# Sending tokens to per-expert regions during the gates instead of gathering them in the routed stage of a one-core ViT tower with a mixture of experts

## The chip, the cores and the metric

One core of one Trainium2 chip runs the whole program in one launch. The metric is the device time of that core in microseconds (us); lower is better. PE is the matrix engine, ACT the activation engine, DVE the vector engine, POOL the GpSimd engine, SP the engine that only issues DMAs here.

## The reference, cut to what matters

64 images give 64 x 49 = 3136 tokens of width 128. After a patch embedding, a layer norm and an S4 convolution comes the part that the change touches, a feed-forward layer with 2 shared and 8 routed experts (hidden width 512). Each token goes to its two best experts.

```python
hs = gelu(einsum('td,nfd->ntf', t, sw1) + sb1)            # 2 shared experts, all tokens
shared = einsum('ntf,ndf->td', hs, sw2) + sb2.sum(0)
logits = t @ gate_w.T + gate_b
probs = softmax(logits); top_v, top_i = top_k(probs, 2)
cw = zeros_like(probs).at[arange(T)[:, None], top_i].add(top_v)
hr = gelu(einsum('td,efd->etf', t, rw1) + rb1)            # 8 routed experts
oe = einsum('etf,edf->etd', hr, rw2) + rb2
out = h + shared + einsum('etd,te->td', oe, cw)
```

## The kernel before, in words

Tokens are held 98 to a group (two images, `PAIR`), 32 groups (`NPAIR`); four groups make a chunk of 392 tokens (`GT`), and there are 8 chunks (`NG`). All engines have a program of their own, written out by hand, and meet through semaphores alone; each engine runs its own in order.

The feed-forward layer is a list of 48 units in a fixed order (`ORDER`, lines 77 to 83). 16 are shared units (one chunk by one shared expert), 32 are routed units, called blocks here: 256 slots that belong to one expert (`NB` = 32, `BLK` = 256). The first 12 units are shared; then come the blocks, with one more shared unit behind every sixth block.

PE works one unit ahead (L1523 to L1550): in step q it does the up-projection of unit q+1 (`up`, L1443), transposes the gathered tokens of the block after that (`transpose_in`, L1508), and then does the down-projection of unit q (`down_shared` L1462, `down_routed` L1473). ACT does the gelu between them (L765). DVE copies the transposed tokens out (`keep_x`, L1145) and adds the bias to a block's result (`rows_out`, L1151, tile `og`). A down-projection of block i waits for `og` of block i-1.

The tokens' way before the change: the normalised tokens `ym` of each chunk are stored to a DRAM table `yd` by SP (`store_y`, L469). In the steps up to q = 3, PE multiplies each chunk with the gate weights (`gate`, L1430). When all eight chunks are done, DVE computes softmax, picks the two best experts and gives each (token, expert) pair a slot (`gate_logits`, `gate_probs`, `gate_second`, `sort_places`, L1033 to L1115), with one pair of matmuls in between (`count_places`, L1493). Slots are then turned into index lists by one-hot matmuls (`one_hots` L1117, `invert` L1500, `slot_tokens` L1128): `take` says which token a slot takes, `give` to which row of the DRAM table `rd` its result goes. POOL then gathers 128 tokens per indirect DMA, two per block, up to four blocks ahead (`gather`, L605), and scatters the results, again two per block (`scatter`, L613). POOL's order is: gathers of blocks 0 to 3, then for each i the gathers of block i+4 and the scatters of block i (L620 to L628). A gather waits until its buffer's earlier tokens have been transposed, a scatter for `og`.

SP loads each block's expert weights from a copy in SBUF, `wba` (up, 258 KB) and `wbb` (down, 320 KB), three blocks ahead (`load_weights`, L474). Before `wbb` of block i+3 it waits for `og` of block i. At the end SP loads the routed rows back (`load_routed`), ACT and DVE weigh and add them (`scale_routed`, `combine`), and SP stores the output.

Before its first up-projection, DVE waits for constants that POOL makes (`sort_constants`, L578).

## Time and profile before

| what | us |
|---|---|
| median of three runs | 507.42 (505.32 to 509.38) |
| the profiled execution, own time | 508.58 |
| its span, first to last instruction | 506.8 |
| PE busy | 386.9 (76%) |
| ACT busy | 208.2 (41%) |
| POOL busy | 193.4 (38%) |
| DVE busy | 183.7 (36%) |

The span is what the rows below divide; the own time lies 1.8 us above it. The shares are averages over stages with different limits: patch embedding and convolution up to about 185 us, shared units with the gates to about 283 us, the routed stage to about 478 us, and the combination and store of the output to the end.

### The profile page before, as it was taken

The numbers are of one execution on the slowest core, as the hardware profiler recorded it, in microseconds if no ns is written. First come the engines' busy times: TensorE is split into PE (matmuls) and PEld (weight loads), VectorE is DVE, ScalarE is ACT, GpSimd is POOL, SyncE is SP. The second block draws the span as 40 slices with busy tenths as digits, with TensorE's granted clock in tenths as the row PEclk, the third lists the DMA queues.
The fourth block names the chain that finished last, engine by engine and source line by source line (L and its number), as shares of the span: only waits on it lengthen the run. The fifth ranks groups of instructions, "written<-read, shape, count | busy, mean of one in ns | idle before, by whom it ended". The sixth has DMA issues, their size and how long they took to land.

```text
span 506.8 us, 7360 instructions
## 1 busy us (share of the span) xinstructions
PE 386.9 (76%) x2561; PEld 313.5 (62%) x2561; DVE 183.7 (36%) x564; ACT 208.2 (41%) x423; POOL 193.4 (38%) x254
## 2 busy tenths in 40 slices
PE   0869998999589754999699978888596797696600
PEld 0648666666367643877589677777396496496600
DVE  0661858486930354435861111111021111121146
ACT  2641758463352143766333322424232342342243
POOL 6050262624110025400003466676546666556600
PEclk9995999999779795999988997999798998998955
DMA  9950349300225102110201234344334343444176
GB/s 222 262 160 2 97 120 321 118 1 10 87 77 167 45 1 65 32 34 1 104 38 18 55 130 141 136 141 176 90 119 140 125 147 135 134 130 136 70 210 176
DMA packets 35240, 55.43 MB, mean 109 GB/s; under 512 B 5431, under 2 KB 20397, under 8 KB 35209
## 3 DMA queue, kind: packets, MB, share of 16 engines
q1 hardware_dynamic: 30185, 46.25, 28.7%
q0 software_dynamic: 4480, 8.46, 6.6%
q10 hardware_dynamic: 544, 0.33, 0.3%
q8 instruction: 17, 0.28, 0.2%
q14 instruction: 14, 0.11, 0.1%
HBM read 28.63 MB, written 7.46 MB: 71 GB/s over the span
## 4 chain that ended last, share of the span: by engine, by line
PE 34%; issue 30%; DVE 10%; POOL 6%; POOLq 6%; DMA 5%; another core or an unknown queue 4%; ACT 3%; SPq 1%; DVEq 1%; ACTq 0%
PE bank L1459 12%; PE bank L1481 11%; PE bank L1469 4%; DVE dT L822 3%; DMA out<-osb 2%; DMA gbb<-in_L_ffn_gate_b 2%; ACT gf L765 2%; PE bank L1504 2%; POOLq L598 1%; POOL QT L566 1%; PE bank L1515 1%; POOLq L548 1%; POOL rstd L544 1%; DVE xtok L871 1%
## 5 line engine op out<-in xcount | busy, mean ns | idle before, releaser
L765 ACT ACTIVATE gf<-bank,wba 128x256 f32<-128x256 f32 x128 | 55.2, 474 | 99.0 <-remote 45.5
L610 POOL DMA_INDIRECT xg<-yd,take x64 | 62.5, 977 | 76.9 <-DVE give L1143 57.7
L617 POOL DMA_INDIRECT rd<-og,give x64 | 63.4, 990 | 63.3 <-DVE og L1155 47.1
L1481 PE MATMUL bank<-wbb,gf 128*128 128x128 f32 x512 | 69.1, 293 | 23.2 <-issue 23.1
L1481 PEld LDWEIGHTS bank<-wbb,gf 128*128 128x128 f32 x512 | 65.4, 206 | 25.5 <-issue 25.5
L1459 PE MATMUL bank<-x,wba 128*128 128x256 f32 x256 | 67.5, 406 | 14.0 <-issue 12.5
L1459 PEld LDWEIGHTS bank<-x,wba 128*128 128x128 f32 x256 | 49.4, 205 | 25.2 <-issue 17.0
L765 ACT ACTIVATE gf<-bank,vcol 128x392 f32<-128x392 f32 x64 | 34.7, 589 | 52.2 <-PE bank L1441 33.7
L1155 DVE TENSOR_TENSOR og<-bank,wbb 128x256 f32<-128x256 f32 x32 | 13.6, 424 | 101.8 <-remote 67.1
L1469 PE MATMUL bank<-gf,ws 128*128 128x392 f32 x128 | 45.1, 495 | 0.0
L1254 PE MATMUL bank<-patchT,Wp 128*128 128x392 f32 x96 | 37.4, 515 | 0.0
L1149 DVE COPY x<-bank 128x256 f32<-128x256 f32 x32 | 13.6, 424 | 60.6 <-PE bank L1515 30.2
L1469 PEld LDWEIGHTS bank<-gf,ws 128*128 128x128 f32 x128 | 23.5, 190 | 13.4
L1439 PE MATMUL bank<-yh,ws 128*128 128x392 f32 x64 | 25.8, 404 | 3.5 <-DVE yl L1013 3.5
L1221 PE MATMUL bank<-ident,Xr 112*128 112x112 f32 x168 | 23.7, 285 | 5.9 <-ACT patchT L643 4.0
L1221 PEld LDWEIGHTS bank<-ident,Xr 112*128 112x128 f32 x168 | 19.5, 154 | 11.4 <-issue 6.3
L643 ACT COPY patchT<-bank 128x448 f32<-128x448 f32 (+1 forms) x48 | 21.2, 490 | 7.0 <-PE bank L1221 6.7
L1440 PE MATMUL bank<-yl,ws 128*128 128x392 f32 x64 | 23.6, 368 | 0.0
L1441 PE MATMUL bank<-yh,ws 128*128 128x392 f32 x64 | 23.3, 365 | 0.0
L654 ACT COPY Xr<-Xc 112x1792 f32<-112x1792 f32 x12 | 20.3, 1688 | 6.5 <-DMA Xc<-in_x 6.5
L1254 PEld LDWEIGHTS bank<-patchT,Wp 128*128 128x128 f32 x96 | 17.2, 199 | 7.6 <-issue 1.1
L1377 PE MATMUL bank<-Tt,u 98*32 98x98 f32 x256 | 19.9, 481 | 2.5 <-DMA Tt<-kpad 2.5
(242 smaller groups left out, 617.0 us busy)
## 6 DMA issues: line engine op xcount, KB each, us to landing
wbb<-stb SPq DMA_DIRECT2D x32, 320.0 KB
Xc<-in_x SPq DMA_DIRECT2D x12, 784.0 KB, 6.6
wba<-sta SPq DMA_DIRECT2D x32, 258.0 KB
rk<-rd SPq DMA_DIRECT2D x16, 196.0 KB
Tt<-kpad SPq DMA_DIRECT2D x8, 300.1 KB
raw<-in_L_ffn_rw SPq DMA_DIRECT2D x1, 2048.0 KB, 10.6
yd<-ym SPq DMA_DIRECT2D x8, 196.0 KB
out<-osb SPq DMA_DIRECT2D x8, 196.0 KB
```

The costliest lines, as they stand in the source:

```text
L610: G.indirect_dma_start(out=xg[i % AHEAD][:, t, :], out_offset=None, in_=yd[:, :], in_offset=bass.IndirectOffsetOnAxis(ap=take[:, at:at + 1 ...
L617: G.indirect_dma_start(out=rd[:, :], out_offset=bass.IndirectOffsetOnAxis(ap=give[:, at:at + 1], axis=0), in_=og[i % 2][:, t, :], in_offse ...
L643: nc.scalar.copy(patchT[:, t, lo:hi, :].rearrange("p w r -> p (w r)"), bank[i][:, 0:(hi - lo) * TR]).then_inc(tp_copied[i], 1)
L765: nc.scalar.activation(gf[q % 2][:, o, 0:width(q)], bank[o][:, 0:width(q)], ACT.Gelu, bias=bias1(n, o)).then_inc(act_done, 1)
L1221: return TP(dst, src, ident[0:rows_, 0:rows_])
L1254: last = MM(bank[2 + half][:, 0:GT], Wp[:, t, :], patchT[:, t, :, half * HR:(half + 1) * HR], start=t == 0, stop=t == KT - 1)
L1439: MM(dst_, hi_w, hi_x, start=start, stop=False)
L1440: MM(dst_, hi_w, lo_x, start=False, stop=False)
L1441: return MM(dst_, lo_w, hi_x, start=False, stop=stop)
L1459: last = MM(bank[o][:, 0:BLK], wba[i % WB][:, FO + o * 128:FO + (o + 1) * 128], x32[i % 2][:, :], start=True, stop=True)
L1469: last = MM(bank[4][:, 0:GT], ws2[:, n % NS, o * D:(o + 1) * D], gf[q % 2][:, o, :], start=begin and o == 0, stop=last_ and o == FO - 1)
L1481: last = MM(bank[7][:, D * t:D * (t + 1)], gf[q % 2][:, o, 128 * t:128 * (t + 1)], wbb[i % WB][:, o * D:(o + 1) * D], start=o == 0, stop=o ...
```

## The change

The gates are worked on in four rounds of two chunks. As soon as a round's tokens have their experts, POOL scatters them to DRAM: each expert has a region of 3392 rows in a new table `xd`, and a token's row in it is its rank among that expert's tokens. Two indirect DMAs of 98 rows per group, 64 in all, take the place of the 64 gathers of 128 rows. In the routed stage SP loads a block's 256 tokens, which are consecutive rows of one region, with one plain DMA (`load_tokens`), whose start row it reads from `rowint`. `store_y`, `yd`, `take` and the gathers go. `ym` has eight buffers instead of four, so that a chunk stays until it is sent. DVE's slot numbering is split into `choose`, `send` (rounds 0 to 3), `number_slots` (step 5) and `shares` (step 10); the one-hot steps come one step later. SP also writes 256 rows of zeros behind each region's tokens (`pad_rows`). PE's `gate` of chunks 2, 4 and 6 waits for DVE. The order of the units is the same.

```diff
+S_NUMBER = 5
+S_HOT = 6
+S_TURN = 9
...
-            for c in range(NG):
-                store_y(c)
+            def load_tokens(i):
+                at = sp_.value_load(rowint[0:1, i:i + 1], min_val=0, max_val=E * TT - BLK)
+                if i == 0:
+                    sp_.wait_ge(st_pad, 16 * E)
+                    for g in range(NGR):
+                        sp_.wait_ge(dispatched[g], 16 * 2 * GPP)
+                if i >= AHEAD:
+                    sp_.wait_ge(tin_done, i - AHEAD + 1)
+                sp_.dma_start(xg[i % AHEAD][:, :, :], xd[bass.ds(at, BLK), :].rearrange("(t p) d -> p t d", t=TILES_OF)).then_inc(ld_xg[i % AHEAD], 16)
...
+            for e in range(E):
+                pad_rows(e)
             sp_.wait_ge(w_hi, 2 * NX)
             sp_.wait_ge(biases_in, 1)
+            for i in range(WB):
+                load_weights(i)
+            for i in range(WB - 1):
+                load_tokens(i)
             for i in range(NB):
-                load_weights(i)
+                if i + WB - 1 < NB:
+                    load_tokens(i + WB - 1)
+                if i + WB < NB:
+                    load_weights(i + WB)
...
                 G.memset(nothing[:, :], 0.0)
+                G.memset(zrows[:, :, :], 0.0)
+                G.memset(keep[:, :, 1:GPP + 1], 1.0)
+                for i in range(2):
+                    G.memset(run[i][:, :, 0:1], 0.0)
+                for e in range(E):
+                    G.memset(base_of[:, e:e + 1], float(e * TT))
+                G.memset(keep[:, :, 0:1], 0.0)
...
-            def gather(i):
+            def dispatch(g):
+                pool.wait_ge(row_ready, g + 1)
+                for c in range(GC * g, GC * (g + 1)):
+                    for p in range(GP):
+                        for k in range(2):
+                            at = GP * c + p
+                            G.indirect_dma_start(out=xd[:, :], out_offset=bass.IndirectOffsetOnAxis(ap=xrow[:, k, at:at + 1], axis=0),
+                                                 in_=ym[c][:, p, :], in_offset=None).then_inc(dispatched[g], 16)
...
+            for g in range(NGR):
+                dispatch(g)
             pool.wait_ge(idx_ready, 1)
-            for i in range(4):
-                pool.wait_ge(st_y[i], 16 * NG // 4)
-            for i in range(AHEAD):
-                gather(i)
             for i in range(NB):
-                if i + AHEAD < NB:
-                    gather(i + AHEAD)
                 scatter(i)
...
+            def choose(g):
+                ps = slice(GPP * g, GPP * (g + 1))
+                b = g % 2
+                dve.wait_ge(gate_done, GC * (g + 1))
+                V.tensor_tensor(lg[:, ps, :], ...).then_inc(lg_read, 1)
+                pick(0, lg[:, ps, :], ps)
+                V.scalar_tensor_tensor(pr[:, ps, :], hots[:, 0, ps, :], -3e38, lg[:, ps, :], ALU.mult, ALU.add)
+                pick(1, pr[:, ps, :], ps)
...
+                V.tensor_copy(cum[b][:, :, :], run[b][:, :, :]).then_inc(sel_ready, 1)
+
+            def send(g):
+                dve.wait_ge(rank_T, g + 1)
+                V.tensor_tensor(ranks[:, :, ps], bank[7]..., base_of..., ALU.add)
+                V.tensor_tensor(held[:, :, :, :], hots[:, :, ps, :], ranks..., ALU.mult)
+                V.tensor_reduce(pos[:, :, ps], held[:, :, :, :], AX.X, ALU.add)
+                V.tensor_copy(xrow[:, :, ps], pos[:, :, ps]).then_inc(row_ready, 1)
...
-                if q == NG // 2 - 1:
-                    gate_logits()
-                    gate_probs()
-                    gate_second()
-                    sort_places()
+                if 1 <= q <= NGR:
+                    send(q - 1)
+                if q < NGR:
+                    choose(q)
+                if q == S_NUMBER:
+                    number_slots()
...
             def gate(c):
                 pe.wait_ge(yh_ready, c + 1)
+                if c % GC == 0 and c >= GC:
+                    pe.wait_ge(lg_read, c // GC)
+                if c >= 2 * GC and c % GC == 0:
+                    pe.wait_ge(row_ready, c // GC - 1)
...
             def transpose_in(i):
-                pe.wait_ge(gathered[i % AHEAD], 16 * TILES_OF * (i // AHEAD + 1))
+                pe.wait_ge(ld_xg[i % AHEAD], 16 * (i // AHEAD + 1))
...
+                if 1 <= q <= NGR:
+                    count(q - 1)
+                if q == NGR + 1:
+                    count_all()
```

## Rows read from the trace of the kernel before

**Rows 1.** Busy time in the shared units, the routed stage, and one stall of it (header first)
```profile
core 0: us, PE busy (x) PEld busy (x) DVE busy (x) ACT busy (x) POOL busy (x), PEclk, DMA share, GB/s
200.00:283.00 83.00, 77.58 (x404) 63.55 (x403) 40.17 (x115) 40.10 (x78) 14.39 (x24) 0.93 0.15 44
283.00:478.00 195.00, 158.55 (x929) 137.18 (x930) 27.77 (x65) 65.60 (x147) 115.39 (x118) 0.93 0.38 128
...
300.00:316.00 16.00, 11.69 (x62) 10.53 (x60) 1.60 (x4) 3.38 (x8) 10.65 (x11) 0.79 0.35 121
```
**Rows 2.** Who waited for whom, 283 to 478 us: total us, times, longest us
```profile
DVE og L1155 <- remote: 67.1, 12, 7.4
ACT gf L765 <- remote: 58.7, 13, 7.1
...
PE bank L1481 <- issue: 23.1, 9, 4.1
```
**Rows 3.** Timeline of PE, 293.4 to 306 us: start, duration, line, operation, count
```profile
293.57 0.38 PE L1515 MATMUL bank<-ident,xg 128*128 128x128 f32 x2
293.79 1.95 PE L1481 MATMUL bank<-wbb,gf 128*128 128x128 f32 x16
295.58 1.89 PE L1459 MATMUL bank<-x,wba 128*128 128x256 f32 x8
...
297.52 1.95 PE L1481 MATMUL bank<-wbb,gf 128*128 128x128 f32 x16
299.31 1.89 PE L1459 MATMUL bank<-x,wba 128*128 128x256 f32 x8
301.04 0.38 PE L1515 MATMUL bank<-ident,xg 128*128 128x128 f32 x2
305.54 0.77 PE L1481 MATMUL bank<-wbb,gf 128*128 128x128 f32 x2 [4.12 <-issue]
```
**Rows 4.** Timeline of DVE, the same stretch
```profile
295.78 0.42 DVE L1155 TENSOR_TENSOR og<-bank,wbb 128x256 f32<-128x256 f32 x1 [1.36 <-issue]
...
305.01 0.42 DVE L1155 TENSOR_TENSOR og<-bank,wbb 128x256 f32<-128x256 f32 x1 [6.72 <-remote]
```
**Rows 5.** Timeline of POOL, 270 to 325 us
```profile
284.43 0.94 POOL L610 DMA_INDIRECT xg<-yd,take  x1 [0.30 <-issue]
293.35 1.01 POOL L617 DMA_INDIRECT rd<-og,give  x1 [7.98 <-DVE og L1155]
...
302.40 0.97 POOL L610 DMA_INDIRECT xg<-yd,take  x1 [0.30 <-issue]
305.71 1.00 POOL L617 DMA_INDIRECT rd<-og,give  x1 [2.34 <-DVE og L1155]
```
**Rows 6.** Groups of instructions of POOL over the span: busy us, mean ns
```profile
L617 POOL DMA_INDIRECT rd<-og,give x64 | 63.4, 990 | 63.3 <-DVE og L1155 47.1 <-issue 16.2
L610 POOL DMA_INDIRECT xg<-yd,take x64 | 62.5, 977 | 76.9 <-DVE give L1143 57.7 <-issue 19.2
...
L518 POOL DMA_DIRECT2D we<-in_L_tok_W_embed x1 | 0.5, 511 | 0.0
L534 POOL MEMSET rev<- 98x1 f32 x8 | 0.3, 113 | 0.0
```
**Rows 7.** Timeline of PE, 184 to 292 us: shared units, then the first block
```profile
233.69 2.79 PE L1469 MATMUL bank<-gf,ws 128*128 128x392 f32 x8
238.90 2.79 PE L1469 MATMUL bank<-gf,ws 128*128 128x392 f32 x8
...
281.63 0.38 PE L1515 MATMUL bank<-ident,xg 128*128 128x128 f32 x2
282.91 1.99 PE L1459 MATMUL bank<-x,wba 128*128 128x256 f32 x8 [0.90 <-DVE x L1149]
```
**Rows 8.** Timelines of DVE, SP's queue and ACT, 472 to 507 us
```profile
478.40 0.42 DVE L1155 TENSOR_TENSOR og<-bank,wbb 128x256 f32<-128x256 f32 x1 [2.16 <-PE bank L1481]
...
482.68 4.76 SPq L491 DMA_DIRECT2D rk<-rd  x8
...
486.11 1.28 ACT L779 ACTIVATE scl<-rk,cwk 98x128 f32<-98x128 f32 x4 [11.93 <-DMA rk<-rd]
```
**Rows 9.** Timeline of SP's queue, 293.4 to 309 us
```profile
305.55 0.49 SPq L481 DMA_DIRECT2D wbb<-stb  x1
306.73 0.49 SPq L478 DMA_DIRECT2D wba<-sta  x1
```
**Rows 10.** Timeline of POOL, 194 to 200 us
```profile
196.77 0.30 POOL L588 MEMSET nothing<- 98x256 f32 x1
197.02 0.17 POOL L589 MEMSET allone<- 98x98 bf16 x1
```
**Rows 11.** Timeline of DVE in the gates, 184 to 262 us
```profile
209.30 0.57 DVE L1013 TENSOR_TENSOR yl<-y,yh 128x392 fp32r<-128x392 f32 x1 [2.43 <-ACT yh L757]
217.59 0.57 DVE L1013 TENSOR_TENSOR yl<-y,yh 128x392 fp32r<-128x392 f32 x1 [1.24 <-ACT yh L757]
...
249.12 0.20 DVE L1108 CAST posi<-pos 98x64 int32<-98x64 f32 x1
249.39 0.20 DVE L1110 TENSOR_SCALAR posq<-posi 98x64 int32<-98x64 int32 x1
```
**Rows 12.** Chain of work that ended last: start us, us, what
```profile
480.38 2.24 DMA rd<-og,give
```
**Rows 13.** Gathers by tile: duration ns min/median/max, first and last start us
```profile
L610 POOL DMA_INDIRECT xg<-yd,take x64: 943/970/1147, 273.0 to 464.6; - x64
```
**Rows 14.** Timeline of ACT, 281 to 287 us
```profile
283.65 1.34 ACT L765 ACTIVATE gf<-bank,wba 128x256 f32<-128x256 f32 x3 [4.30 <-PE bank L1459]
286.38 0.47 ACT L765 ACTIVATE gf<-bank,wba 128x256 f32<-128x256 f32 x1 [1.39 <-PE bank L1459]
```

More of the change, by code:

```diff
@@ L74 @@
 RKS = 4
+TT = T + BLK
+GC = 2
+NGR = NG // GC
+GPP = GP * GC
 LEAD = 12
@@ L169, in tower @@
         rbb = place("rbb", [128, E, D], "w")
+        zrows = place("zrows", [128, TILES_OF, D], "w")
+        ymw = [place(f"ymw{i}", [PAIR, GP, D], "w") for i in range(4)]
         assert end["w"] <= base + SA, (end["w"] - base, SA)
@@ L245, in tower @@
         Av = [place(f"Av{i}", [PAIR, NQ, JG], "g", F16) for i in range(2)]
-        ym = [place(f"ym{i}", [PAIR, GP, D], "g") for i in range(4)]
-        first = place("first", [PAIR, E, NPAIR], "g")
+        ym = [place(f"ymg{i}", [PAIR, GP, D], "g") for i in range(4)] + ymw
         more = place("more", [PAIR, E, NCNT], "g")
         owner = place("owner", [1, NB, E], "g")
+        offs = place("offs", [1, NB, E], "g")
+        mine = place("mine", [1, E], "g")
         assert end["g"] <= base_h, (end["g"], base_h)
@@ L302, in tower @@
         ld_wb = [sem(f"ld_wb{i}") for i in range(WB)]
-        gathered = [sem(f"gathered{i}") for i in range(AHEAD)]
+        ld_xg = [sem(f"ld_xg{i}") for i in range(AHEAD)]
         scattered = [sem(f"scattered{i}") for i in range(2)]
@@ L307, in tower @@
         st_zero, st_k, st_out = sem("st_zero"), sem("st_k"), [sem(f"st_out{i}") for i in range(2)]
-        st_y = [sem(f"st_y{i}") for i in range(4)]
+        dispatched = [sem(f"dispatched{i}") for i in range(NGR)]
+        st_pad = sem("st_pad")
         lsrep_ready, par_T, ls_T, vec_T = sem("lsrep_ready"), sem("par_T"), sem("ls_T"), sem("vec_T")
@@ new lines, in choose @@
+                V.tensor_tensor(run[b][:, :, 1:GPP + 1], hots[:, 0, ps, :].rearrange("t p e -> t e p"),
+                                hots[:, 1, ps, :].rearrange("t p e -> t e p"), ALU.add)
+                if g >= 1:
+                    V.tensor_copy(run[b][:, :, 0:1], run[1 - b][:, :, GPP:GPP + 1])
+                dve.drain()
+                V.tensor_tensor_scan(run[b][:, :, :].rearrange("t e p -> t (e p)"), keep[:, :, :].rearrange("t e p -> t (e p)"),
+                                     run[b][:, :, :].rearrange("t e p -> t (e p)"), 0.0, ALU.mult, ALU.add)
@@ L1087, in sort_places @@
                 dve.drain()
[L1088 removed]
+                V.tensor_tensor_scan(bupto[:, :], blocks[:, :], nothing[:, :], 0.0, ALU.add, ALU.max)
                 dve.drain()
[L1090 to L1091 removed]
+                V.tensor_scalar(last_of[:, :], bupto[0:1, E - 1:E], -1.0, None, ALU.add)
@@ L1101, in sort_places @@
                 dve.drain()
-                for k, to in enumerate((eq, rank)):
-                    V.tensor_tensor(to[:, :, :], hot[k][:, :, :], first[:, :, :].rearrange("t e p -> t p e"), ALU.mult)
+                V.scalar_tensor_tensor(rowint[:, :], colc[:, :], float(BLK), rowsum[:, :], ALU.mult, ALU.subtract).then_inc(own_ready, 1)
+                V.tensor_tensor(ranks[:, :, :], ranks[:, :, :], shiftby[:, :].unsqueeze(2).broadcast_to([PAIR, E, NPAIR]), ALU.add)
                 dve.drain()
-                for k, of_ in enumerate((eq, rank)):
+                for k, to in enumerate((eq, tie)):
+                    V.tensor_tensor(to[:, :, :], hots[:, k, :, :], ranks[:, :, :].rearrange("t e p -> t p e"), ALU.mult)
@@ L1106, in sort_places @@
+                dve.drain()
+                for k, of_ in enumerate((eq, tie)):
                     V.tensor_reduce(pos[:, k, :], of_[:, :, :], AX.X, ALU.add)
```

180 lines of the change are left out of this document (94 added, 86 removed).

## Prediction

> **What bounds the kernel now.** First the stretches [rows 1]: with the shared units PE is busy 77.6 of 83 us, so that stage is PE's own. The routed stage is the longest, 195 us with PE busy 158.6; POOL is busy 115.4 there. Next, the waits of the routed stage [rows 2]: the largest are DVE's `og` and ACT's gelu on a releaser that the profile does not know ("remote"), 67 and 59 us, and PE stands for 23 us before down-projections. The timelines show one such stall. A block costs PE 3.73 us when nothing holds it (down at 293.79, next at 297.52) [rows 3]. The third is due at 301.3, but starts at 305.54 [rows 3], because `og` of the block before runs at 305.01 [rows 4], although its matmuls ended near 299.5. POOL had then issued eight indirect DMAs in a row, 293.35 to 303.37 [rows 5], and DVE is released 1.6 us behind their end. Four indirect DMAs at about 0.98 us each and 0.30 between [rows 5, 6] are 5.1 us per block, more than PE's 3.73. So POOL's DMAs pace the routed stage: the 32 blocks and four shared units at 5.21 [rows 7] need 32 x 3.73 + 20.8 = 140.2 us of PE, and with the 2.6 of the down-projection begun before, 143. From the first up-projection at 282.91 [rows 7] to `og` of the last block at 478.40 [rows 8] they take 195.5.
>
> **The change, part by part.** All sums are made in the profiled execution.
>
> *Gathers gone.* POOL's load falls to two scatters, 2.6 us per block [rows 6]. The stalls above go: up to 195.5 - 143 = 52 us. What is late next is the load of tokens.
>
> *Token loads.* SP issues `load_tokens(j)` right behind both weight loads of block j, and `wbb` of block j waits for `og` of block j-3. PE's order is down(j-3), up(j-1), transpose(j), down(j-2). The load must therefore land within one up-projection, about 1.7 us [rows 3]. It cannot. From a transpose to the end of `og`: 293.57 to 296.20 = 2.63 us [rows 3, 4]. SP picks up 0.1 us later, issues `wbb`, and its next DMA follows 1.18 us behind [rows 9]. The load itself, 128 KB in pieces of 512 B behind 320 KB on the same queue, is not in the trace. Nearest is the pair of `rk` loads, 392 KB in such pieces: issued from 482.68, used at 486.11, so 3.4 us [rows 8]. For 448 KB, the smaller part issued 1.18 us late, I take 3.7 from the issue of `wbb`, with 3.4 and 4.4 as ends (the latter if the tokens need another 3.2 of their own). The cycle is closed: transpose, down, `og`, `wbb`, tokens, transpose = 2.63 + 0.1 + 3.7 + 0.05 = 6.5 us (6.2 to 7.2), against 3.73. Who waits: PE, with the down-projection queued behind the transpose. The first three blocks are loaded ahead; the two behind each of the four shared units have the slack of that unit. This leaves 32 - 3 - 8 = 21 waits of 2.77 us = 58.2 us. Routed stage: 143 + 58 = 201 us, against 195.5: +5.5 (-1 to +20).
>
> The Trainium skill (DMA: Bandwidth & Descriptors, Anatomy of one DMA) fits a DMA from GpSimd as 2.0 us plus bytes over 436 GB/s, 2.3 us for 128 KB. If that held for SP's load behind its weights, the cycle would be 2.63 + 0.1 + 1.18 + 2.3 = 6.2 us and the result 6 us lower; `rk` speaks for the longer one.
>
> *Constants.* POOL makes some 13 more memsets, one of 128x256, before DVE may begin; one of 98x256 costs 0.25 from start to start [rows 10]. Eight of 98x1 take 0.3 together [rows 6]. I take +0.8 us (0.3 to 1.5) and nothing hides it.
>
> *Gates.* `choose` is 16 or 17 DVE operations on 98x64 elements, 0.27 us apart [rows 11]: 4.4 us; `send` is four, 1.3 us. The first `choose` stands behind `low_y(2)`, which ends at 209.87 [rows 11], and ends at 215. All later work of DVE in step 1 shifts by 5.2, `low_y(4)` from 217.59 [rows 11] to about 223, with half a microsecond for the norms that wait on POOL. The first `send` is done at 225. PE's new waits (`lg_read`, `row_ready`) hold gate 4 and what is queued behind it some 7 us, and later ones a few more. Numbering in step 5 and one-hots one step later put the index lists at about 283 and the first transposes at 285, against 281.63 [rows 7]. This alone would cost 4 us; it is hidden behind the next part.
>
> *Dispatch.* 64 indirect DMAs of 98 rows, back to back from 225: every later `row_ready` comes sooner than POOL needs it. One of 128 rows takes 0.98 [rows 6]; a plain POOL DMA of few rows 0.51 [rows 6]. Between these by rows: 0.51 + 0.47 x 98/128 = 0.87, with 0.30 of gap 1.17 (0.81 to 1.28). 64 x 1.17 = 75 us, so POOL ends at 300; the last one lands 1.3 behind its end (2.24 from a start of 0.97 length) [rows 12]. `load_tokens(0)` waits for all of them, and needs 0.1 and some 2.5; transpose to up-projection is 1.28 [rows 7]. First up-projection at about 305.4, against 282.91 [rows 7]: +22.5. With 0.81 the dispatch ends at 277 and the index lists decide: +4. With 1.28: +30. Earlier no part of the routed stage can start, since only 12 units precede it. PE stands about 19 us; before, a stand of 4.1 us [rows 3] was followed by work at the lower level of the clock, 1.2 GHz (granted 0.79 in the mean of that stretch) [rows 1], so I add 1.5.
>
> The Trainium skill (SBUF — State Buffer, Who interferes with whom) says that a DVE operation in a two-port mode locks GpSimd out of writing its descriptors. In this trace the gathers vary little (0.94 to 1.15 us over 64) [rows 13]. If each of some 20 casts and copies of the new gates held up one DMA by its own 0.2 us, dispatch would end 4 us later.
>
> *Nothing from the rest.* `store_y` went beside the gates on a queue without other work; the pads (1 MB) run beside the shared units. The end is unchanged: two scatters, `rk`, combination, 28.4 us.
>
> *Sum.* 22.5 + 1.5 + 5.5 = +29.5. (The 0.8 of the constants is in the 22.5.) Span 506.8 + 29.5 = 536.3, own time 1.8 more, 538.1. The profiled execution of before (508.58) was 1.2 above its median, so against the median: **537 us**.
>
> **Rivals.**
> *The long run of indirect DMAs holds PE's signals (572 us, chance 0.25).* For: after eight in a row DVE and ACT saw PE's signals up to 5.5 us late [rows 2 to 5]; in the first run of ten gathers the fourth gelu got its signal at 286.38 [rows 14], 1 us after that run's end at 285.37 [rows 5]. Against: up to 283.65, eight gathers into that run, the gelus before it came on time [rows 14]. If PE's signals stop some 8 us into the dispatch, its first two rounds hold PE for about 30 us, and the next rounds then wait for PE: the last round ends near 312 with six or seven shared units left, first up-projection about 340. That is +35 on the forecast.
>
> *The routed stage runs free (479 us, chance 0.06).* This is the other side. Were the token loads in time, which needs them to land within 1.7 us of the down-projection's end, the 21 waits would be nothing: 305.4 + 143 = 448 at the last `og`, 30 before the present 478.4, and 537 - 58 = 479. It decides from a landing of about 1.2 us behind `og`; against it stands every load in the trace.
>
> *Both new costs small (511 us, chance 0.12).* Dispatch at 0.81 per DMA and cycles of 6.2: 4 + 0.8 - 1 = +3.8, so 511. The chance of ending within 1% is half of this.
>
> *Scatters alone still hold PE's signals (558 us, chance 0.07).* Then some one microsecond more for each of the 21 waits: 537 + 21. For: scatters are half of the runs that held the signals; against: two in a row are 2.6 us, followed by a pause of four.
>
> **How the numbers follow.** Forecast 0.50: 537, its own range 526 to 548. The high end takes in the held signals, 580; the low end the small costs, 511. A measurement of this kernel can tell about 1% from no change. Faster by over 1%: 0.06 for free running and 0.01 beside it; within 1%: 0.06; slower: 0.87.
>
> **What would show it.** Right: POOL issues 64 `xd` DMAs from about 225 to 300; the first routed up-projection at about 305; between blocks PE waits 2 to 3 us before the transpose of `xg`, with the DMA of `xg` as releaser, in about 21 places, and not behind shared units; no "remote" waits of DVE and ACT. Wrong: PE gaps inside the dispatch (held signals), or blocks 3.7 us apart (loads in time), or a dispatch DMA far from 0.87.

## The result, and the profile of the changed kernel

The changed kernel takes 596.71 us in the median of four runs (593.16 to 606.83), the kernel before beside it 508.4 us: ratio 1.171, 95% interval 1.158 to 1.184. The direction was forecast, the size was not: 537 us with a range to 580. In this document the times are medians of all executions, while a ratio leaves out those that were over 1.5% slower than the fastest of the same kernel.

The profiled execution is the longest of the four (606.83, span 605.0; it reaches the shared units some 6 us later than the profile of before), so positions below are some microseconds late. Its stretches in windows (busy time per engine, PE's granted clock, DMA share, GB/s), for [rows 1]:

```profile
core 0: us, PE busy (x) PEld busy (x) DVE busy (x) ACT busy (x) POOL busy (x), PEclk, DMA share, GB/s
205.00:363.00 158.00, 90.61 (x411) 71.07 (x411) 54.17 (x194) 40.61 (x79) 68.35 (x80) 0.72 0.13 41
363.00:575.00 212.00, 160.91 (x914) 140.33 (x914) 28.60 (x67) 66.73 (x147) 57.45 (x60) 0.92 0.33 118
575.00:605.00 30.00, 2.02 (x16) 1.86 (x16) 14.77 (x42) 10.22 (x32) 3.83 (x4) 0.60 0.60 170
```

The stretch of the shared units has grown from 83 us [rows 1] to 158, and PE is busy for only 91 of them; the routed stage from 195 to 212. Most of the excess lies ahead of the first block. PE's timeline there, its longest waits from the first `lg` on and the first routed up-projection (start, duration, operation, in brackets the idle time before it and its releaser), for [rows 7]:

```profile
230.13 1.47 PE L1508 MATMUL bank<-gwT,y 128*98 128x8 f32 x8 [6.78 <-DVE lg L1088]
276.43 1.50 PE L1508 MATMUL bank<-gwT,y 128*98 128x8 f32 x8 [32.07 <-ACT yh L795]
...
305.93 0.69 PE L1513 MATMUL bank<-yh,ws 128*128 128x392 f32 x1 [2.88 <-issue]
325.59 5.60 PE L1543 MATMUL bank<-gf,ws 128*128 128x392 f32 x8 [18.31 <-ACT acc L809]
363.75 1.56 PE L1533 MATMUL bank<-x,wba 128*128 128x256 f32 x6 [0.90 <-DVE x L1216]
```

Two halts, 32.07 and 18.31 us, both behind ACT. The 6.78 is the wait for `lg` (the gate's result, which DVE must have read) that the prediction has at "some 7 us". The first routed up-projection is at 363.75 (before 282.91 [rows 7], forecast 305.4). POOL's timeline, the dispatch (answering to [rows 5]):

```profile
230.24 1.13 POOL L655 DMA_INDIRECT xd<-ymg,xrow  x1 [4.62 <-DVE xrow L1121]
231.67 1.00 POOL L655 DMA_INDIRECT xd<-ymg,xrow  x1 [0.30 <-issue]
...
269.75 0.96 POOL L655 DMA_INDIRECT xd<-ymg,xrow  x1 [0.31 <-issue]
279.75 0.95 POOL L655 DMA_INDIRECT xd<-ymw,xrow  x1 [9.05 <-DVE xrow L1121]
...
319.25 0.96 POOL L655 DMA_INDIRECT xd<-ymw,xrow  x1 [0.30 <-issue]
```

Two runs of 32 indirect DMAs without a break, 230.24 to 270.7 and 279.75 to 320.2, 1.26 us from start to start mostly. ACT's timeline beside them, for [rows 14]:

```profile
236.28 0.59 ACT L803 ACTIVATE gf<-bank,vcol 128x392 f32<-128x392 f32 x1 [0.32 <-PE bank L1515]
275.50 0.48 ACT L794 COPY y<-bank 128x392 f32<-128x392 f32 x1 [37.88 <-remote]
...
295.38 0.59 ACT L803 ACTIVATE gf<-bank,vcol 128x392 f32<-128x392 f32 x1 [8.90 <-remote]
305.29 0.59 ACT L803 ACTIVATE gf<-bank,vcol 128x392 f32<-128x392 f32 x1 [3.64 <-remote]
324.95 0.59 ACT L809 ACTIVATE acc<-bank,sb2s 128x392 f32<-128x392 f32 x1 [19.07 <-remote]
```

ACT serves PE promptly up to 236.28, six microseconds into the first run; then it stands for 37.88 us on a releaser that the profile does not know, and goes on 4.8 us behind the run's end, while PE had stopped at 244.4 for want of ACT's result. What the copy at 275.50 waits for are matmuls of PE that ended at 242.18, as PE's timeline has it:

```profile
241.68 0.50 PE L1291 MATMUL bank<-ident,ymw 98*128 98x98 f32 x4
```

So PE's signal took 33.3 us to reach ACT. It is the pattern of [rows 3 to 5], forty microseconds long: PE works, its signals don't arrive, and PE in the end waits for engines that wait for PE. The hold is not total: in the second run ACT is served at 295.38, 298.21, 301.06 and 305.29, in its middle, and then stands until 324.95, again 4.7 us behind the run's end.

The waits of the routed stage came as foretold: 21 of them. Their sums (us in total, times, longest):

```profile
PEld bank L1598 <- DMA xg<-xd: 58.5, 21, 3.6
PE bank L1598 <- DMA xg<-xd: 50.1, 21, 3.2
```

And one turn of the cycle in two timelines, PE's first (for [rows 3]) and SP's queue behind it (for [rows 9]):

```profile
383.94 0.44 PE L1598 MATMUL bank<-ident,xg 128*128 128x128 f32 x2 [2.33 <-DMA xg<-xd]
390.12 0.44 PE L1598 MATMUL bank<-ident,xg 128*128 128x128 f32 x2 [2.22 <-DMA xg<-xd]
```

```profile
386.75 0.49 SPq L494 DMA_DIRECT2D wbb<-stb  x1
387.98 0.39 SPq L524 DMA_DIRECT2D xg<-xd  x1
```

In this turn it is 6.18 us from transpose to transpose; PE begins with the tokens 2.14 us behind their issue and 3.37 behind that of `wbb`. Other turns take 7.2 us and more; what makes them longer is shown in the last part.

### The profile page after: what moved, and what is told of

It reads as the page before. It is cut to its first block, busy times and chain, and to the rows that moved or that the text cites. A ratio compares the mean times of both kernels' runs of the same rounds, so it can differ in the third digit from the quotient of the medians.

```text
span 605.0 us, 7754 instructions
## 1 busy us (share of the span) xinstructions
PE 405.9 (67%) x2568; PEld 326.3 (54%) x2568; DVE 197.5 (33%) x639; ACT 209.9 (35%) x424; POOL 191.0 (32%) x267
## 4 chain that ended last, share of the span: by engine, by line
PE 32%; issue 22%; DMA 12%; another core or an unknown queue 10%; DVE 7%; SPq 5%; POOL 5%; POOLq 4%; ACT 2%; DVEq 1%; ACTq 0%
PE bank L1557 11%; DMA xg<-xd 8%; PE bank L1543 7%; PE bank L1533 3%; DVE dT L861 3%; PE bank L1598 2%; SPq L494 2%; PE bank L1513 2%; DMA gbb<-in_L_ffn_gate_b 2%; DMA out<-osb 2%; PE bank L1515 2%; PE bank L1514 2%; DVE og L1222 2%; SPq L517 2%
## 5 line engine op out<-in xcount | busy, mean ns | idle before, releaser
L1557 PE MATMUL bank<-wbb,gf 128*128 128x128 f32 x512 | 75.4, 311 | 0.6 <-issue 0.6
L1557 PEld LDWEIGHTS bank<-wbb,gf 128*128 128x128 f32 x512 | 73.2, 227 | 0.8 <-issue 0.7
L1543 PE MATMUL bank<-gf,ws 128*128 128x392 f32 x128 | 50.7, 544 | 18.3 <-ACT acc L809 18.3
L1598 PE MATMUL bank<-ident,xg 128*128 128x128 f32 x64 | 14.8, 317 | 50.1 <-DMA xg<-xd 50.1
L1598 PEld LDWEIGHTS bank<-ident,xg 128*128 128x128 f32 x64 | 7.7, 150 | 59.5 <-DMA xg<-xd 58.5
L1508 PE MATMUL bank<-gwT,y 128*98 128x8 f32 x64 | 8.5, 260 | 43.4 <-ACT yh L795 35.9
L655 POOL DMA_INDIRECT xd<-ymw,xrow x32 | 31.0, 969 | 18.5 <-issue 9.4
L1513 PE MATMUL bank<-yh,ws 128*128 128x392 f32 x64 | 27.8, 435 | 12.5 <-issue 7.0
L655 POOL DMA_INDIRECT xd<-ymg,xrow x32 | 31.0, 969 | 14.1 <-issue 9.4
L1508 PEld LDWEIGHTS bank<-gwT,y 128*98 128x98 f32 x64 | 8.1, 210 | 45.9 <-ACT yh L795 37.4
```

What stands on the lines that cost most here:

```text
L655: G.indirect_dma_start(out=xd[:, :], out_offset=bass.IndirectOffsetOnAxis(ap=xrow[:, k, at:at + 1], axis=0), in_=ym[c][:, p, :], in_offset ...
L1513: MM(dst_, hi_w, hi_x, start=start, stop=False)
L1543: last = MM(bank[4][:, 0:GT], ws2[:, n % NS, o * D:(o + 1) * D], gf[q % 2][:, o, :], start=begin and o == 0, stop=last_ and o == FO - 1)
L1557: last = MM(bank[7][:, D * t:D * (t + 1)], gf[q % 2][:, o, 128 * t:128 * (t + 1)], wbb[i % WB][:, o * D:(o + 1) * D], start=o == 0, stop=o ...
L1598: last = TP(bank[6][:, 128 * t:128 * (t + 1)], xg[i % AHEAD][:, t, :], ident[:, :])
```

## The experiments

A sitting is a group of kernels measured together, on one chip and beside runs of before. Five sittings fell into two kinds, which turned out to be the main thing: before took about 508 us in two of them and about 476 in three, all kernels of a sitting alike. One chip gave the one kind in the second sitting and the other in the fourth. "Held" and "on time" below are these two kinds, after what the traces show of PE's signals. The first result is of the held kind.

| kernel | before 508, held | before 476, on time |
|---|---|---|
| before | 508.2 to 509.7 | 475.6 to 476.2 |
| before, only the first gathers (e4, e9) | | 459.9, 459.4 |
| after (first result, r_after, r_after_again) | 596.7, 594.8 | 554.2 |
| after without the dispatch (e5, e1) | 536.8 | 537.3 |
| after, plain POOL DMAs (e7) | 539.0 | |
| after, pause every 4 (e6, e3) | 571.0 | 572.2 |
| after, pause every 8 (e8) | 590.9 (three of six at 581, three at 600 to 605) | |
| tokens earlier (e2) | | 492.1 (485.2 to 495.0) |
| tokens earlier, 16 shared first (x1, x7) | 531.2 | 469.7 |
| the same, pause every 4 (x2) | 487.8 | |
| the same, pause at the rounds' ends too (x4) | | 487.4 |
| x1 with drain and memset, drain alone (x5, x6) | | 502.3, 500.5 |

### First sitting (on time): e1 to e4

e1: no dispatch.

```diff
-            for g in range(NGR):
-                dispatch(g)
...
+            sp_.dma_start(xd[0:GT, :].rearrange("(p i) d -> i p d", p=GP), ym[0][:, :, :]).then_inc(dispatched[0], 16)
...
-                V.scalar_tensor_tensor(rowint[:, :], colc[:, :], float(BLK), rowsum[:, :], ALU.mult, ALU.subtract).then_inc(own_ready, 1)
+                V.scalar_tensor_tensor(rowint[:, :], colc[:, :], 0.0, rowsum[:, :], ALU.mult, ALU.mult).then_inc(own_ready, 1)
```

> After without POOL's 64 indirect DMAs of the tokens: one chunk's tokens are stored by SP, every block reads these same 256 rows, so the output is not the reference's; all waits of the gates among PE, DVE and ACT, all numbering, pads, token loads and scatters stay. Theory (the long runs of POOL's indirect DMAs hold PE's signals back, and that alone halts PE for 32 and 18 us): both halts are gone, PE stays busy through the shared units, the first routed up-projection is at 288 to 297 us instead of 363.75, and the time is near 596 - 70 = 526 (518 to 535). Rival (the new waits among PE and DVE in the four rounds of gates halt PE, whatever POOL does): first routed up-projection later than 330, time 570 or more.

e2: tokens one block earlier.

```diff
-            for i in range(WB - 1):
+            for i in range(WB):
                 load_tokens(i)
             for i in range(NB):
-                if i + WB - 1 < NB:
-                    load_tokens(i + WB - 1)
+                if i + WB < NB:
+                    load_tokens(i + WB)
                 if i + WB < NB:
                     load_weights(i + WB)
```

> After with one edit: SP issues the token load of block i+3 ahead of block i+3's weights and not behind them, one block earlier than before. Theory (the cycle transpose, down-projection, og, weights, tokens, transpose costs PE 21 waits of about 2.77 us): these waits go, blocks follow each other in 3.7 to 4.2 us, the routed stage is 50 to 58 us shorter, time 538 to 548. Rival (POOL's two scatters per block, or the weights, pace the stage as well): waits move to another releaser, blocks stay above 5 us, time above 570. Without the 21 waits the scatters could hold PE's signals: then DVE and ACT show waits without a known releaser and the gain is 20 to 40 us.

e3: a pause in the dispatch (the expression for n is written out in the kernel and shortened here).

```diff
+                            # n = number of this DMA in its round, from 1 to 16
+                            if n < 2 * GPP and n % 4 == 0:
+                                pool.wait_ge(dispatched[g], 16 * n)
```

> After with one edit: within a round POOL waits after every fourth indirect DMA until that DMA has landed. The dispatch itself gets longer: 64 x 1.26 + 16 x about 1.5 = 105 us. Theory (what holds PE's signals is that POOL issues many indirect DMAs without a pause; groups of four with a pause let them through): no halt of PE longer than about 6 us, the index lists come in time, the dispatch ends near 335 and decides; first routed up-projection 340 to 350, time 575 to 585. Rival (the number of indirect DMAs or the time that POOL spends on them counts, pauses or not): PE halts for as long as in after or longer, first up-projection at 365 to 390, time 598 to 625.

e4: before without most gathers.

```diff
             def gather(i):
+                if i < AHEAD:
...
-                pe.wait_ge(gathered[i % AHEAD], 16 * TILES_OF * (i // AHEAD + 1))
+                pe.wait_ge(gathered[i % AHEAD], 16 * TILES_OF)
```

> Before with the gathers of all blocks but the first four left out (later blocks work on the tokens of these, so the output is not the reference's); scatters, weights and order of units stay. Theory (POOL's four indirect DMAs per block, 5.1 us, pace the routed stage of before, and with two per block PE runs at 3.73 us a block): routed stage 143 to 155 us instead of 195.5, time 455 to 468. Rival (two scatters a block still hold PE's signals): blocks at 4.5 us or more, time 480 to 495. Rival (the low clock or the weights bound the stage): time above 495.

Measured: 537.25, 492.12, 572.19 and 459.87 us, with before at 476.22 (ratios 1.132, 1.030, 1.209, 0.972). None of the four traces has a wait on an unknown releaser, not even e2's, where the dispatch is unchanged. So e1 and e3 said nothing yet of the hold; the controls of the next sitting were made for that. What they did say:
- e2: the 21 waits are gone, as the theory has it, and scatters and weights keep up. The routed stage, first up-projection to last `og`, takes 146.5 us (319.0 to 465.5). Only the load's place in SP's order was in the way. The 538 to 548 expected was reckoned from after with its halts, which this sitting does not have.
- e1: the gates alone, without any dispatch, put the first up-projection at 303.1, later than the 288 to 297 expected, and the time, 537, lies just above its 518 to 535.
- e3: its dispatch decides, as expected, but ends at 326.9 and not near 335, first up-projection 331.7 for 340 to 350, time below its 575 to 585.
- e4: the blocks run at PE's pace. Gathers cost before 16 us in this kind of sitting, not 52. (No trace of before itself was taken in a sitting on time.)

### Second sitting (held): controls, and the dispatch taken away again

> The kernel before, unchanged, as a control beside the others: in the call of e1 to e4 it took 476 us where it had taken 507, and the traces of those kernels show each PE signal 0.01 us behind its matmul all through the dispatch. Theory (PE's signals are held behind runs of POOL's indirect DMAs only in some executions or on some chips): the time says which kind this is. If about 476: no wait on a releaser that the profile does not know, PE timed by POOL's four indirect DMAs per block alone, routed stage 163 to 168 us (32 x 5.1). If about 507: stalls as in the trace before.

> The changed kernel, unchanged, as a control. Theory (the excess of 597 over the forecast of 537 is the held signals alone): where before takes about 476, after has no halts of PE of 32 and 18 us in the dispatch, first routed up-projection 318 to 322, 21 waits for tokens of 2.5 to 2.8 us, time 535 to 548, ratio 1.13 to 1.15; where before takes about 507, the halts are there again, time 590 to 605, ratio 1.17. Rival (the halts come from the new waits of the gates): halts there wherever it runs.

> e1 again, now beside after in one call: after without POOL's 64 indirect DMAs of the tokens (every block reads the same 256 rows, so the output is not the reference's). Theory: where signals are held (before about 507), no halt of PE in the shared units, and 60 to 75 us less than after; where they are not (before about 476), the routed stage starts at 303 and not at 319, so 10 to 18 us less than after, and the 21 waits stay. Rival (the new waits of the gates): halts of PE also here.

x1 is e2's edit and `LEAD = 16` for `LEAD = 12`.

> Two edits to after: the tokens' loads one block earlier (e2) and all 16 shared units ahead of the first block. Theory (in e2 PE stood 17 us before the first transpose, and the four late shared units cost 20.8 us; they fill that stand): first up-projection still about 319, routed stage 32 x 3.73 = 120 us, 16 to 19 us less than e2: ratio to before 0.98 to 1.00 where signals come on time. Rival (the dispatch gets slower beside more PE work, or the four units gave the tokens' loads slack that is now gone): 5 us or less gained on e2, ratio 1.02 or more. Where signals are held: ratio 1.05 or more.

Measured: 509.74, 594.83 (ratio 1.175, 1.168 to 1.182), 536.83 (1.059) and 531.24 (1.049). r_after halts at the same places as the first profile, waits of r_after from the page of waits:

```profile
ACT y L794 <- remote: 37.7, 1, 37.7
DVE h L1064 <- remote: 32.5, 2, 27.6
ACT acc L809 <- remote: 19.8, 1, 19.8
```

In the same sitting the kernel without the dispatch has no such wait at all, PE's longest ones are 6.78 and 4.12 us, and the first routed up-projection comes at 301.29 and not at 357.68:

```profile
227.60 1.47 PE L1507 MATMUL bank<-gwT,y 128*98 128x8 f32 x8 [6.78 <-DVE lg L1087]
266.54 0.67 PE L1512 MATMUL bank<-yh,ws 128*128 128x392 f32 x1 [4.12 <-ACT gf L802]
```

Its time is 537 in both kinds of sitting, and here 58 us less than after's, where 60 to 75 was expected. The new waits of the gates are therefore not what halts PE; the 64 indirect DMAs are. x1 keeps both halts (32.04 and 14.85 us): it is 64 us faster than after, and still slower than before.

### Third sitting (held): what in the dispatch holds the signals

> e3 again (after, POOL waits for landing after every fourth indirect DMA of the dispatch). In e3's call PE's signals came on time anyway, so it told nothing of the hold; here the time of before tells the kind: about 508 with held signals, about 476 without. Where they are held: theory (a pause after four lets the signals through) no halt of PE over 6 us, dispatch ends near 328, first routed up-projection near 332, time 570 to 580 against 595 for after. Rival (total of indirect DMAs counts, pauses or not): halts of 20 us or more stay, time 595 to 620. Where they are not held: 572 as before.

e7:

```diff
-                            G.indirect_dma_start(out=xd[:, :], out_offset=bass.IndirectOffsetOnAxis(ap=xrow[:, k, at:at + 1], axis=0),
-                                                 in_=ym[c][:, p, :], in_offset=None).then_inc(dispatched[g], 16)
+                            G.dma_start(xp[PAIR * (2 * at + k):PAIR * (2 * at + k + 1), :], ym[c][:, p, :]).then_inc(dispatched[g], 16)
```

> After with POOL's 64 indirect DMAs of the dispatch turned into 64 plain ones of the same 98 rows and the same source tiles, to fixed rows of a table of its own; every block reads one chunk's first 256 rows, so the output is not the reference's. Theory A (what holds the signals is the indirect form): where before takes 508, no halt of PE in the dispatch, routed stage from about 301 as in the kernel without a dispatch, 537 us. Theory B (any long run of POOL's own DMAs does it): halts of 10 to 32 us, time 560 to 600. Price of one plain DMA of 98 rows: 0.5 to 1.0 us on POOL.

> All three edits to after: tokens' loads one block earlier, all 16 shared units first, POOL's pause after every fourth indirect DMA of the dispatch. Theory where signals are held (before 508): dispatch ends near 328, shared units done by 322, first up-projection near 333, routed stage 120 to 126 us, end 28.4 behind: 482 to 490 us, ratio 0.95 to 0.97. Where they are not (before 476): 484, ratio 1.01 to 1.03. Rival (pauses don't help): 531 or more where held.

e8 is e3's edit with 8 for 4.

> After with the pause after every eighth indirect DMA: how long may a run be? In the trace of before the hold begins within runs of eight. Theory (a run of eight already holds for some 3 to 5 us, and the pause of about 1.5 us lets go): where held, PE loses 3 to 5 us in each of eight runs, partly hidden, dispatch ends near 325, time 565 to 590, between after and the pause every 4. Rival (the hold needs a longer run than eight): same halts as with four, time 8 to 12 us below it, about 562. Where not held: about 560.

Measured: 570.95 (ratio 1.126), 539.0 (1.063), 487.8 (0.950, 0.943 to 0.958) and 590.9 (1.145).

e7: PE has no longer waits in the gates than without a dispatch (6.77 and 4.17 us), and 539 is about the time without one (537), though 64 DMAs of the same rows go out back to back from 227 to 263. Its tile `xp` (durations in ns, minimum, median, maximum):

```profile
L660 POOL DMA_DIRECT2D xp<-ymg x32: 559/559/687, 227.1 to 245.1; - x32
L660 POOL DMA_DIRECT2D xp<-ymw x32: 559/559/562, 245.6 to 262.7; - x32
```

So neither "POOL issues DMAs" nor this amount of data holds the signals; the indirect form does. Whether it does so by its longer time on POOL (0.96 us for 0.56) or by rows that go to scattered places is not separated. e6: POOL's timeline shows the pauses, and the waits of ACT on unknown releasers (second fence) shrink from 37.7 to 5.4:

```profile
231.82 0.96 POOL L655 DMA_INDIRECT xd<-ymg,xrow  x1 [1.54 <-DMA xd<-ymg,xrow]
238.31 1.01 POOL L655 DMA_INDIRECT xd<-ymg,xrow  x1 [1.55 <-DMA xd<-ymg,xrow]
```

```profile
ACT y L796 <- remote: 5.4, 1, 5.4
ACT acc L811 <- remote: 4.5, 1, 4.5
```

Apart from the wait for `lg`, PE's longest one before it stands for the tokens is 3.1 us, and the time is the same in both kinds: 571 here, 572 on time. Twelve pauses of about 1.55 us cost less than they free. They shorten the hold and don't remove it. The two waits shown end at 237.59, behind a run of four, and at 257.00, behind one of eight (the rounds have no pause at their ends, so there eight stand in a row). In x2 one gelu starts at 293.34, 6.9 us behind its matmuls. No kernel without any run of eight was measured where signals are held; x4, which has none, ran on time.

e8 (expected 565 to 590) fell into two: three executions at 581 us, 10 above e6 and 14 under r_after, and three at 600 to 605, longer than after's. Its trace is of the longest, 605.55, so the halt below is shown for these alone. The edit does less than its name says. It has no pause at a round's end, and the next round's rows are ready, so POOL's timeline shows pauses only before DMAs 9, 25, 41 and 57, runs of 8 and of 16; behind two of these rows the waits:

```profile
237.85 0.96 POOL L655 DMA_INDIRECT xd<-ymg,xrow  x1 [1.54 <-DMA xd<-ymg,xrow]
259.50 0.96 POOL L655 DMA_INDIRECT xd<-ymg,xrow  x1 [1.57 <-DMA xd<-ymg,xrow]
```

```profile
DVE ranks L1115 <- remote: 33.1, 3, 26.6
ACT acc L811 <- remote: 17.2, 1, 17.2
```

Four pauses inside a dispatch are not enough when sixteen DMAs follow three of them: in this execution PE halts for 26.7 us once more. Why the others were 20 us shorter is not known, and where between eight and sixteen in a row the cost begins is not settled.

x2 is the first version that beats before where signals are held: 128 us for the 32 blocks, at a granted clock of 0.98:

```profile
334.00:462.00 128.00, 125.26 (x842) 114.77 (x842) 27.42 (x65) 57.16 (x129) 59.46 (x63) 0.98 0.55 197
```

### Fourth sitting (on time): scatters alone, and other kinds of pause

> e4 again (before with the gathers of all blocks but the first four left out; later blocks work on the tokens of these, so the output is not the reference's), hoped to run where signals are held (before about 508). Theory (two scatters a block, with a pause behind them, don't hold PE's signals; the 508 of before is four indirect DMAs per block in runs of eight and more): 458 to 466 us as in e4, ratio 0.90 to 0.92. Rival (scatters alone hold them, one us or more per block): 485 or more.

x4 drops `n < 2 * GPP` from the condition of the pause.

> x2 (tokens one block earlier, 16 shared units first, pause after every fourth dispatch DMA) with a pause behind the last DMA of each of the four rounds too, where x2 still has runs of eight. Theory (runs of eight hold PE for some us, but PE's end of the shared units at 324.7 has 8 us of slack to the tokens at 333): three pauses of 1.5 us more in the dispatch, no long wait on an unknown releaser left in the shared stage, time 2 to 6 us above x2: 486 to 494. Rival (held signals still cost x2 time): 476 to 483.

x5 (x6 without the last line), both on top of x1:

```diff
+                            if n % 4 == 0:
+                                pool.drain()
+                                G.memset(spare[:, :], 0.0)
```

> x1 (tokens earlier, 16 shared first) where POOL drains and does a memset of 98x256 (0.25 us) after every fourth dispatch DMA and does not wait for landing. Theory A (any piece of other work on POOL between indirect DMAs lets the signals through): no halts where signals are held, dispatch 88 us, time 476 to 484. Theory B (POOL must be without an indirect DMA for longer, more than 0.5 us): halts of 15 to 32 us as in x1, time 525 to 540.

> The same with the drain alone and no memset. Theory A: 474 to 482. Theory B: halts as in x1, 525 to 540 us where signals are held. If x5 is free of halts and this one is not, it is the work on POOL and not the drain that lets them through.

Measured: 459.4 (ratio 0.963), 487.36 (1.025), 502.33 (1.056), 500.52 (1.048), before 475.63. The sitting was of the other kind than hoped, so of the three open questions it closes none by itself. e9 repeats e4: 143.4 us from the first up-projection (286.98) to the last `og` (430.39), the 143 of the prediction. That two scatters per block cost little where signals are held, x2 shows instead: 127.0 us for the blocks (334.2 to 461.2) against 123.9 of x7, with two waits on unknown releasers in the stage, 3.9 and 1.0 us. x5 and x6 missed by 20 us for a reason of their own: a drain behind four indirect DMAs stands longer than a wait for landing, 2.25 us before the next start and not 1.55, in POOL's timeline of x6:

```profile
229.62 0.95 POOL L656 DMA_INDIRECT xd<-ymg,xrow  x1 [0.30 <-issue]
232.83 0.96 POOL L656 DMA_INDIRECT xd<-ymg,xrow  x1 [2.25 <-issue]
```

Whether it is the landing or any interruption that lets the signals through stays open. x4 came out at 487.36, within its 486 to 494; what its three further pauses do where signals are held is not measured.

### Fifth sitting (on time): after by itself, and x1 again

> The changed kernel unchanged, once more, hoped for a call in which before takes about 476 (signals not held). Theory: no halt of PE in the dispatch, first routed up-projection 318 to 322, 21 waits for tokens, 535 to 548 us, ratio 1.13 to 1.15. Rival: another cost beside the held signals, so above 555. Where before takes about 508: 590 to 600 again.

> x1 again (tokens one block earlier, 16 shared units first, dispatch without pauses). Where before takes about 476: dispatch ends near 314, the shared units near 322, first up-projection 323 to 326, 470 to 480 us, ratio 0.99 to 1.01. Where it takes about 508: 531 as in x1.

Measured: 554.23 (ratio 1.161, 1.152 to 1.170) and 469.69 (0.984, 0.976 to 0.992), before 476.24. r_after_again has no halt in the dispatch. The same copy of ACT that stood for 37.88 us in the first profile starts here 0.04 us behind the same matmuls (PE's timeline and ACT's):

```profile
238.22 0.50 PE L1291 MATMUL bank<-ident,ymw 98*128 98x98 f32 x4
238.76 0.49 ACT L794 COPY y<-bank 128x392 f32<-128x392 f32 x1 [3.89 <-PE bank L1291]
```

Its time is above the 535 to 548 expected, although the first up-projection is early (318 to 322 expected). Its later PE rows and, behind them, its windows:

```profile
266.38 0.67 PE L1513 MATMUL bank<-yh,ws 128*128 128x392 f32 x1 [4.32 <-ACT gf L803]
314.81 0.69 PE L1598 MATMUL bank<-ident,xg 128*128 128x128 f32 x2 [13.96 <-DMA xg<-xd]
316.02 3.78 PE L1533 MATMUL bank<-x,wba 128*128 128x256 f32 x8 [0.52 <-DVE x L1216]
```

```profile
199.00:316.00 117.00, 85.51 (x411) 69.84 (x411) 55.81 (x200) 40.82 (x79) 72.63 (x96) 0.81 0.18 55
316.00:530.00 214.00, 162.27 (x930) 140.84 (x930) 28.17 (x66) 66.80 (x147) 59.09 (x62) 0.92 0.33 118
```

PE stands 13.96 us for the tokens, whose last dispatch DMA starts at 310.17. And x7, the best on time (a shade under the 470 to 480 expected), in windows: PE works 123.27 of 124.5 us at the full clock.

```profile
320.50:445.00 124.50, 123.27 (x842) 113.01 (x842) 27.37 (x64) 57.05 (x129) 59.36 (x62) 1.00 0.56 201
```

## Why the prediction was wrong, step by step

**The step that failed** is *Dispatch*, in its sentence "64 indirect DMAs of 98 rows, back to back from 225 ... PE stands about 19 us": it let PE go on working beside the run, with nothing but the stand for the tokens behind it. Where the signals are held, PE halts for 32 and 18 to 19 us inside it, the shared units end late, and the first up-projection comes at 357.7 (r_after) where the same kernel in a sitting on time has it at 316.0. That is 41.7 us of the first up-projection and 40.6 us of the time (594.8 against 554.2): 51.0 us of halts take the place of the 13.96 for the tokens, and some 5 are shorter waits and slower work. It was the rival "The long run of indirect DMAs holds PE's signals", given 0.25. It had the mechanism and the place, and was too small: "about 30 us" against 50 in the two halts together, first up-projection 340 against 357.7. Its counter-argument, that eight gathers had gone by before a gelu was late, holds in the trace of after too (ACT is on time for six microseconds) and weighs nothing in a run of 32. The rows to weigh it by were there: [rows 2] has 126 us of such waits in a stage with runs of eight, and the forecast puts 64 in a row.

The whole difference where signals are held, in the profile of r_after (span 594.5 for the 536.3 of the sum, +58.2): the first up-projection comes 52.3 us late, the routed stage takes 210.1 for 202.5 (+7.6, with the 1.5 added for the clock), and the end is 1.7 shorter.

**Where signals are on time** the forecast of 537 stands against 554.2, in the profile of r_after_again a span of 557.6 for the 536.3 of the sum, +21.3:
- *Start of the routed stage*, 316.0 for 305.4: +10.6. The first `send` frees POOL at 227.4 and not 225; but the shared units also begin later in this execution, at 202.7 for 199.2 in the trace of before, and only 0.5 of that are the new constants (0.8 forecast). A dispatch DMA takes 0.957 us (median) for 98 rows, as much as the 0.98 of 128 [rows 6], and not 0.87; the scaling by rows was the wrong choice, its own upper bound of 1.28 per turn the right one. 83.7 us for all 64 instead of 75. In them are 3.4 us by which single DMAs are longer than 0.956, near the 4 that the prediction reckoned if DVE's casts and copies held POOL up. Apart from one of 1.69, the longest (1.63, 1.43, 1.43 and 1.21) stand beside other operations of DVE, the comparisons and one-hots of L1167 to L1194. That DVE causes them is not shown.
- *Token loads*: at the full clock a turn is 6.2 us, for 6.5 forecast and 6.2 as the low end; 21 waits as counted, 51.1 us of PE's standing for the 58.2 forecast. In the turn shown above PE had the tokens 2.14 us behind SP's issue. By that the fit of the Trainium skill (DMA: Bandwidth & Descriptors, Anatomy of one DMA), cited in the prediction with 2.3 and made for DMAs from GpSimd, was nearer than the `rk` rows from which the 3.7 was taken.
- *Routed stage*, 214 us for 201: +13, or +11.5 with the 1.5 that the prediction adds for the clock, and this although the waits came out 7 us short. The 143 of PE's own work assumed the full clock. In this stage of after the granted clock is 0.92 and PE's busy time 162.3; in e2, same order of units without the waits, it is 145.7 at 0.98. So 16.6 us are slower work at the lower clock. It comes in some turns and not in others, after waits of the same length: 11 of the 21 take 6.1 to 6.3 us, nine take 7.2 to 8.0, and one 6.7. The same down-projection in two turns that follow each other, at 1.95 and at 3.23 us (r_after_again, PE's timeline):

```profile
381.22 1.95 PE L1557 MATMUL bank<-wbb,gf 128*128 128x128 f32 x16
387.73 3.23 PE L1557 MATMUL bank<-wbb,gf 128*128 128x128 f32 x16
```

  The granted clock from 380.95 to 387.2 is 0.98; from 373.14 to 380.9, a turn with a down-projection of 3.53 us, it is 0.78. The term for the clock, +1.5 and once only, was mis-sized. Before pays it as well (158.6 us busy at 0.93, [rows 1]): it was in view.
- *The end*: 27.6 us from the last `og` to the end of the span, 28.4 forecast.

**Gates.** "This alone would cost 4 us; it is hidden behind the next part". It was hidden, but it costs 14 us: from the first shared up-projection to the first routed one e5 takes 98.8 us (202.5 to 301.3), e9, with before's gates, 84.9 (202.1 to 287.0). PE stands for 13.4 us in this stretch where it stood for 5.8 (new are 6.8 for `lg`, as forecast, and 4.1 for ACT, which was not), and works 85.4 us at a granted clock of 0.85 where it worked 79.1 at 0.92. The hiding is gone as soon as the dispatch gets cheap: e5's 537 is this and the 21 waits.

**What was right.** No "remote" waits in the routed stage, blocks 6.2 us apart where the clock was full, tokens' DMA as the releaser in 21 places and not behind shared units. *Scatters alone still hold PE's signals* fell: x2's 32 blocks take 127.0 us, 4.0 each, where signals are held. *The routed stage runs free* fell for after, but e2 made it true, not by a faster landing, which that rival had as its condition, but by an issue one block earlier: its 479 compares with e2's 492. *Gathers gone, up to 52 us*: the 143 is what e2, e4 and e9 show. The cost of the gathers depends on the kind of sitting: 16 us on time (476 to 459.9). For held sittings no run of before without gathers exists; 508 to 459 would be 49 if e4 were unmoved by the kind, as e5 is. That is an inference.

**In the end** the ratio is nearly the same in both kinds, 1.17 and 1.16, by different sums, so this agreement is chance. On time, before has no stalls to be freed from, and after loses in the 21 waits (62 us, r_after_again to e2) and in the start. Where those two are mended the idea gains something, but no version measured beats before in both kinds. Without pauses it is 0.984 on time (x7) and 1.049 held (x1): the same kernel, 470 and 531. With pauses it is 0.950 held (x2) and 1.025 on time (x4, with three pauses more between its DMAs). x2 and x4 lie at 488 and 487, so the pauses look like the steadier choice; neither ran in both kinds, only the pauses without the other edits did (e3 and e6, 572 and 571).

## What to carry to other kernels

A prefetch is as early as what stands ahead of it in its issuing queue: put the load that gates the next step before the one with slack, and count the turn of the cycle (21 waits and the lower clock beside them were 62 us here, gone with three changed lines). A wait of PE of a few microseconds can cost twice, once standing and once in slower work behind it (here 51 and 17 us for the 21), so size PE's own work from its busy time at the clock that the stage is granted. Long unbroken runs of indirect DMAs on GpSimd beside matmuls that other engines must follow are a risk to be priced by their length, and a wait for landing behind every four was a cheap bound here.

## What the runs showed of the hardware

- In some sittings PE's semaphore signals reach ACT and DVE late while POOL issues indirect DMAs in a long unbroken run: a copy of ACT starts 33.3 us behind the matmuls that it waits for, 4.8 us behind the end of a run of 32; where signals are on time it is 0.04. (Behind runs of eight DVE goes on after 1.6 us, [rows 4, 5].) Plain DMAs from POOL, 64 in a row at 0.56 us, don't do it. Pauses of 1.55 us behind every fourth, with runs of eight between rounds, leave ACT waits of up to 5.4 us in e6, and they cost no time (571 held, 572 on time).
- In other sittings, once on the same chip, the same kernels show nothing of it. The DMAs' own durations have the same median in both (0.956 and 0.957 us), and no record in the traces says what differs. A trace shows which kind it is by its waits on unknown releasers; the kernel before differs by 32 us between them. This stays open.
- An indirect DMA of 98 rows takes POOL 0.957 us and 0.30 of gap, no less than one of 128 rows; a plain one 0.56.
- 21 waits of PE of 2.2 to 3.3 us in a stage of 214 us left a granted clock of 0.92 in the stage and 17 us more of PE's busy time than without them; the same down-projection took 1.95 us in one turn and 3.23 in the next.
- A drain on POOL behind four indirect DMAs stood 2.25 us, longer than waiting for them to land, 1.55.
